# Stage end without a wait for stores, and another order of block 0, in a two-layer mixture-of-experts kernel

## The reference

```
# conditional part: one of 5 typed experts per sequence, two shared experts
s0, s1 = dense(x, swi[0], swo[0]), dense(x, swi[1], swo[1])
eo = relu(x @ wi[type]) @ wo[type]
gate_in = concat([eo[:, 0], s0[:, 0], s1[:, 0]])      # first token of each sequence
w = softmax(relu(gate_in @ g1) @ g2)                  # 3 weights per sequence
c = eo * w[0] + s0 * w[1] + s1 * w[2]
# then LN -> 16-head attention -> residual -> LN -> top-2 of 8 experts -> residual
```

## Time and profile before

| what | value |
|---|---|
| median of 3 runs | 601.53 us (599.89 to 604.56) |
| profiled execution | 602.28 us, its span 600.5 us |
| granted clock of TensorE, mean | 0.978 of full speed |
| typed experts end, layer one starts | 206 to 209 us |

### The profile page before, as it was taken

One profiled execution on the slowest core, in us unless ns is written; L12 is line 12 of the kernel. 1 busy time (PEld: TensorE's weight loads), 2 busy tenths in 40 slices (PEclk: granted clock), 3 DMA queues, 4 the chain that ended last, 5 costly groups with the idle time before them and its releaser, 6 DMA issues.

```text
span 600.5 us, 18671 instructions
## 1 busy us (share of the span) xinstructions
PE 540.4 (90%) x5852; PEld 464.3 (77%) x5853; DVE 395.9 (66%) x1440; ACT 372.9 (62%) x799; POOL 298.4 (50%) x308
## 2 busy tenths in 40 slices
PE   7979998788999979989999998998888889999991
PEld 3546665478999768778788887887777879999990
DVE  6988988963333324547587775778866546668782
ACT  2457778856666333655556755467777577888870
POOL 1387888651000068232375655257476575545541
PEclk9999999899999998999999999999999799999996
DMA  8931999423333111121453211032322222236364
GB/s 278 377 61 34 397 396 394 166 71 93 103 104 99 54 40 38 28 43 34 164 126 119 60 41 48 24 81 69 82 60 56 55 83 63 73 96 190 91 196 131
DMA packets 75774, 70.81 MB, mean 118 GB/s; under 512 B 26802, under 2 KB 63012, under 8 KB 75300
## 3 DMA queue, kind: packets, MB, share of 16 engines
q1 hardware_dynamic: 67968, 55.34, 29.9%
q0 software_dynamic: 6400, 13.19, 6.8%
q10 hardware_dynamic: 1316, 1.15, 0.6%
HBM read 30.19 MB, written 39.46 MB: 116 GB/s over the span
## 4 chain that ended last, share of the span: by engine, by line
PE 43%; issue 7%; POOL 6%; DVE 5%; DMA 1%; DVEq 1%; ACT 1%; ACTq 0%; POOLq 0%
PE u_py L1771 7%; PE u_py L1933 6%; PE u_pz L1914 6%; PE u_pg L1914 3%; PE u_pf L1933 3%; POOL u_eo_ew L1584 2%; PE u_pg L1814 2%; PE u_pz L1760 2%; PE u_pz L1762 2%; PE u_pg L1822 2%; PE u_pz L1761 2%; POOL rows_dram L1621 1%; PE u_pg L1836 1%; PE u_pe L1786 1%; PE u_pf L1792 1%
## 5 line engine op out<-in xcount | busy, mean ns | idle before, releaser
L1631 POOL DMA_INDIRECT y_dram<-u_hh,v_to x71 | 68.1, 960 | 59.6 <-DVE u_hh L2707 47.8
L1621 POOL DMA_INDIRECT rows_dram<-u_row,u_slots x64 | 62.8, 982 | 47.7 <-DVE u_slots L2577 31.2
L1771 PE MATMUL u_py<-cwo,u_hh 128*128 128x128 f32 x512 | 69.1, 282 | 3.9 <-DVE u_mid L2438 2.0
L1771 PEld LDWEIGHTS u_py<-cwo,u_hh 128*128 128x128 f32 x512 | 63.8, 194 | 8.7 <-issue 6.6
L1933 PE MATMUL u_py<-w,v_h 128*128 x384 | 53.3, 283 | 7.5 <-DVE u_hh L2707 4.3
L1933 PEld LDWEIGHTS u_py<-w,v_h 128*128 128x128 f32 x384 | 47.4, 194 | 10.2 <-issue 10.1
L1914 PE MATMUL u_pz<-v_xT,v_held 128*128 128x128 f32 x384 | 52.7, 283 | 2.7 <-DVE v_h L2687 2.1
L2159 ACT ACTIVATE u_hh<-u_pz 128x512 f32<-128x512 f32 x64 | 37.9, 595 | 27.7 <-PE u_pz L1762 24.8
L2232 ACT ACTIVATE v_held<-w 128x512 f32 x71 | 44.9, 633 | 12.4 <-PE u_pz L1914 3.8
L1914 PEld LDWEIGHTS u_pz<-v_xT,v_held 128*128 128x128 f32 x384 | 48.2, 198 | 3.9 <-issue 3.5
L2239 ACT ACTIVATE v_h<-u_pz,p_bT 128x128 f32<-128x128 f32 x124 | 36.6, 367 | 11.1 <-PE u_pz L1914 9.5
(11 more groups left out here) (386 smaller groups left out, 1493.0 us busy)
## 6 DMA issues: line engine op xcount, KB each, us to landing
rows_dram<-zero SPq DMA_DIRECT2D x1, 17160.0 KB
v_x<-rows_dram SPq DMA_DIRECT2D x71, 65.0 KB
w<-in_mw SPq DMA_DIRECT2D x2, 2048.0 KB
cwt<-in_cw SPq DMA_DIRECT2D x1, 2560.0 KB
xs_dram<-zero SPq DMA_DIRECT2D x1, 2240.0 KB, 13.0
e_xs<-xs_dram SPq DMA_DIRECT2D x35, 64.0 KB, 2.0
eo_dram<-e_y SPq DMA_DIRECT2D x35, 64.0 KB, 1.5
x_dram<-x SPq DMA_DIRECT2D x8, 256.0 KB
```

What stands on the lines that cost most here:

```text
L1621: pool.indirect_dma_start(rows_dram, bass.IndirectOffsetOnAxis(ap=slots[:, q, k, u:u + 1], axis=0), row[:, q, k, u, :], None).then_inc(sen ...
L1631: pool.indirect_dma_start(y_dram, bass.IndirectOffsetOnAxis(ap=vto[t % XR][:], axis=0), vy[:, t % XR, :], None).then_inc(v_sent[t % XR], 16)
L1771: last = nc.tensor.matmul(py[:, u * D:(u + 1) * D], hh[:, e % HR, u * P:(u + 1) * P], cwo[:, m * KF + k], start=(k == 0 and u == 0), stop= ...
```

## The change

Three things are changed. First, the three result buffers of the typed stage and their store semaphores now belong to the whole kernel; SP no longer waits for the stores at the stage's end, and POOL waits for them at the head of layer one, before the gate's gather. PE issues one unread matmul at the stage's end, not two. Second, the gate's gather lands in a buffer of `ew`, so gather(0) no longer waits for the gate's transpose, and POOL's order is gather(0), weigh(0), gather(1), gather(2), weigh(1), gather(3), carried(0), root1(0), weigh(2). Third, the gate's three steps move from step -1 into step 0 on PE and ACT. PE's order in block 0 is now: turn_x(0), an unread matmul, first e0, e1, e2, e3, gate 0, first e4, gate 1, second e0, gate 2, second e1, first e5, second e2, share, second e3, first e6, e7, turn_x(1), second e4, e5, e6, first e8, second e7, first e9, e10; step 1 is as before. ACT's is: ReLU e0, e1, e2, gate copy, ReLU e3, gate ReLU, ReLU e4, exponential, ReLU e5, e6, `high(1)`, ReLU e7, e8. DVE's is unchanged.

```diff
@@ -30,6 +30,7 @@
 TILE_UNROLL = 6
+YR = 3
 ET = (2 * T + E * (P - 1)) // P
@@ -93,9 +94,11 @@
 
-        kept = {"b_sent": ctx.enter_context(nc.semaphore("b_sent"))}
+        kept = {n: ctx.enter_context(nc.semaphore(n)) for n in ["b_sent"] + [f"e_stored{q}" for q in range(YR)]}
         sems, numbers = [ctx.enter_context(ExitStack())], []
         x1t = sb("x1t", [P, S, D])
+        typed_y = sb("typed_y", [P, YR, D])
+        typed_stored = [kept[f"e_stored{q}"] for q in range(YR)]
         ident = sb("ident", [P, P])
@@ -180,11 +183,11 @@
             typed_experts(nc, sb, pb, sem, ident, ones, tri, ln2, type_of_tile, x1_dram, x1t, xs_dram, eo_dram,
-                          cwt[:, 0:B_WO], cwt[:, B_WO:B_SWI], prep, spent)
+                          cwt[:, 0:B_WO], cwt[:, B_WO:B_SWI], prep, spent, typed_y, typed_stored)
         sems[0].close()
...
         layer_one(nc, a, sb, pb, sem, ident, ones, hmask, type_slot, x1t, eo_dram, v_dram, rows_dram, y_dram,
-                  cws, cwo, prep, expert_of_tile, row_of_tile, row_low, row_high, biases, out)
+                  cws, cwo, prep, expert_of_tile, row_of_tile, row_low, row_high, biases, typed_stored, out)
 
@@ -1123,9 +1126,9 @@
 
-def typed_experts(nc, sb, pb, sem, ident, ones, tri, ln2, type_of_tile, x1_dram, x1t, xs_dram, eo_dram, w1, w2, prep, spent):
-
-    U, V, R = TILE_UNROLL, 3, 3
+def typed_experts(nc, sb, pb, sem, ident, ones, tri, ln2, type_of_tile, x1_dram, x1t, xs_dram, eo_dram, w1, w2, prep, spent, y, stored):
+
+    U, V, R = TILE_UNROLL, 3, YR
     HF = FF // 2
@@ -1139,14 +1142,12 @@
         h = sb("e_h", [P, 2, FF], stack=st)
-        y = sb("e_y", [P, R, D], stack=st)
         pT = [pb(f"e_pT{q}", [P, 512], stack=st) for q in range(2)]
...
         w_held = sem("e_w_held", st)
-        stored = [sem(f"e_stored{q}", st) for q in range(R)]
         x_turned, xT_made, a_summed, c_summed, a_made, c_made, y_summed, y_made = (
@@ -1177,8 +1178,6 @@
                 sp.wait_ge(xt_loaded, 16 * NB)
-                for q in range(R):
-                    sp.wait_ge(stored[q], 16 * len(range(q, TT, R)))
 
@@ -1250,8 +1249,7 @@
                 rolled(pe, step, TT, U, 1)
-                for n in range(2):
-                    idle(pT[0], FF)
+                idle(pT[0], FF)
 
@@ -1341,7 +1339,7 @@
 def layer_one(nc, a, sb, pb, sem, ident, ones, hmask, type_slot, x1t, eo_dram, v_dram, rows_dram, y_dram,
-              cws, cwo, prep, expert_of_tile, row_of_tile, row_low, row_high, biases, out):
+              cws, cwo, prep, expert_of_tile, row_of_tile, row_low, row_high, biases, typed_stored, out):
 
@@ -1572,12 +1570,12 @@
             def _(pool):
-                pool.indirect_dma_start(eo[:, 0, 0, :], None, eo_dram,
+                for q in range(YR):
+                    pool.wait_ge(typed_stored[q], 16 * len(range(q, TT, YR)))
+                pool.indirect_dma_start(ew[:, 0, 0, :], None, eo_dram,
                                         bass.IndirectOffsetOnAxis(ap=type_slot[:, 0:1], axis=0)).then_inc(e0_loaded, 16)
...
                 def gather(i):
-                    if i == 0:
-                        pool.wait_ge(g_summed, 1)
                     after(pool, ew_made, i - 1)
@@ -1632,6 +1630,8 @@
                 for i in range(FIRST, NB):
+                    if i == -1:
+                        weigh(0)
                     if ok(i + 2):
@@ -1645,7 +1645,7 @@
                         scatter(i - 3, 0)
-                    if ok(i + 1):
+                    if ok(i + 1) and i != -1:
                         weigh(i + 1)
@@ -1724,11 +1724,11 @@
                 def gate(i, n):
-                    if i != -1:
+                    if i != 0:
                         return
...
                         pe.wait_ge(e0_loaded, 16)
-                        nc.tensor.transpose(pe_[:, 0:B], eo[:, 0, 0, :], ident[:]).then_inc(g_summed, 1)
+                        nc.tensor.transpose(pe_[:, 0:B], ew[:, 0, 0, :], ident[:]).then_inc(g_summed, 1)
                     elif n == 1:
@@ -1954,12 +1954,19 @@
                         first(i, 0, 3)
+                    gate(i, 0)
+                    if ok(i):
                         first(i, 1, 0)
+                    gate(i, 1)
                     if ok(i - 2):
...
                         second(i, 0, 0)
+                    gate(i, 2)
+                    if ok(i):
                         second(i, 0, 1)
+                    if i == 0:
+                        first(0, 1, 1)
                     if ok(i - 2):
@@ -1967,7 +1974,7 @@
                     share(i)
-                    if ok(i):
+                    if ok(i) and i > 0:
                         first(i, 1, 1)
@@ -1989,6 +1996,9 @@
                         attend(i - 2)
+                    if i == 0:
+                        first(0, 1, 3)
+                        turn_x(1)
                     if ok(i):
@@ -1999,13 +2009,13 @@
                         second(i, 1, 1)
-                    if ok(i + 1):
+                    if ok(i + 1) and i != 0:
                         turn_x(i + 1)
...
                         project(i - 2)
-                    if ok(i):
+                    if ok(i) and i > 0:
                         first(i, 1, 3)
@@ -2015,11 +2025,8 @@
                         first(i + 1, 0, 1)
-                    gate(i, 0)
                     if ok(i + 1):
                         first(i + 1, 0, 2)
-                    gate(i, 1)
-                    gate(i, 2)
                 turn_p(NB - 2, 0)
```

## The result

The changed kernel takes 606.74 us (median of 12 runs, 605.68 to 609.56) against 602.31 us for the kernel before. The ratio is 1.0094 with an interval of 1.0073 to 1.0116: 5.7 us slower (4.4 to 7.0). Forecast was 2.5 us slower. The sign was right and the two mechanisms that were forecast came, but the size was more than twice the forecast: one of their terms was too small, and a third cost, a stop of PE further on, was not in the sum. A few executions, in a slower state of the chip, are left out of every ratio and mean.

The account below looks back on a forecast made before the run. It took PE and POOL's list to be tied up to turn_normed(0), with POOL late next. Root +1.0 and clock +1.5 gave +2.5 us: 604.8 profiled, 604.0 us forecast as median, range 599.5 to 607.5.

Parts of the forecast that it names:

- the two mechanisms that were forecast: In block 0, root1(0) on POOL ends 1.0 us later, and PE's clock halves around its long wait, costing 1.5 us.
- The stage's end: At the typed stage's end, SP is done 1.3 us earlier and PE starts layer one 1.3 us earlier (bounds 0 and 1.3).
- POOL's list and the gate: In block 0, `wtok` comes at 218.5 us, 2.4 us earlier; root1(0) ends 19.5 us after it, 1.0 us later than before.
- The clock: Around PE's 8 us wait before turn_normed(0), a half-clock fall of 3.4 us costs 1.5 us (bounds 0 and 3.4).
- a longer fall: Rival: PE's clock fall costs 3.4 us, or also slows block 1's firsts; 606 us, 14%.
- The sum: Whole kernel: +1.0 us for the root and +1.5 for the clock make +2.5 us, nothing added or given back after 240 us.
- The rival that ends faster: PE keeps its lead of 5.0 us in block 0 because POOL's list shortens; 596.5 us, 6%.

Follow-up runs that it names:

- the filled wait: The changed kernel with eight more unread matmuls that PE issues in front of turn_normed(0), where it waits; ratio to the kernel before 1.0040 (1.0014 to 1.0066).
- both moves on POOL: The changed kernel with gather(1) put back in front of weigh(0) and gather(3) moved behind root1(0); ratio to the kernel before 0.9922, again 0.9942.
- the two timed controls: A second unread matmul of 128 columns at the stage's end, added to the changed kernel (1.0100) and to that kernel with gather(1) earlier and gather(3) later (0.9924).
- gather(1) first: The changed kernel with gather(1) put back in front of weigh(0) on POOL; ratio to the kernel before 0.9999 (0.9971 to 1.0027).

## Why the prediction was off

- **The stage's end**: right in its size, 1.1 to 1.3 us of earlier start; the gate's gather gained 0.3 to 0.6. PE's second matmul had to go for it, as said. But the traces with that end show 1.0 to 1.6 us more at PE's stop in block 1, 1.6 in the changed kernel. This cost stood in the sum at nothing. The step that failed is "from 240 us on every list is as before and PE is nearly always busy, so I find nothing that gives the delay back, or adds to it": PE's list is the same from there, yet PE stops longer in it, with one instruction fewer in front. (That this is its place among the instruction fetches is argued, not shown.) The kernel before has such stops as well, 1.70 us behind block 0's attend, 1.01 there and 1.94 us 78 us later; I had not read them.
- **POOL's list and the gate**: right. `wtok` 11.17 us behind PE's start against 11.1 forecast, the root 19.3 behind weigh(0) against 19.5, turn_normed(0) 1.0 us later, counted from the first typed result (66.3 + 30.3 before, 65.2 + 32.5 after), against 1.0. PE's wait was 7.8 for 8.
- **The clock**: the mis-sized term. I took a fall of 3.4 us, the length of the one in block 0 before, and 1.5 us of loss. It began inside the long wait, lasted 10.2 us, covered the first 5.8 us of the work behind the wait and cost 2.7 us, which the filled wait shows by itself. The bound of 3.4 us held it; of the cases listed the rival "a longer fall" (606 us, given 14%) is the nearest. That its time is also near the measured one is in part luck, since it has no stop of 1.6 us in it.
- **The sum**: 1.0 + 2.7 + 1.6 = 5.3 us, in place of 1.0 + 1.5. Measured were 5.7, 4.9 and 5.6. The range of 599.5 to 607.5 held the time.
- **The rival that ends faster** was rightly given little: with POOL's order as changed, PE's lead of 5 us is wasted. With both moves on POOL it is kept: scores(0, 0) comes 6.1 us earlier than before.
- **The rule of the Trainium skill** ("TensorE: Matmul & The Clock Gate", Part 1), that activity alone releases the throttled state and that half of the throttled time is lost, was on the right side: 5.8 us of work at half the clock, 2.7 us lost. Taking the fall's length, 3.4 us, from a wait of 2 us was my error: with the wait of 7.8 us it was 6.8 or 10.2 us in all seven traces.

Left open is whether the timed price of the changed stage end, 1 to 2 us above what the chain up to scores(0, 0) gives, is the stop alone. The traces say so; the two timed controls say so only once the low clock's time is taken off, and within their noise.

## What to carry to other kernels

Before reordering an in-order engine, find the list that the next stage's first step waits for, and count what stands in front of that step in that list; here five microseconds of gathers that nobody needed yet stood in front of a reciprocal root of one microsecond, and moving them gave 0.6 to 0.8% where the change had lost 0.9%. When a reordering gathers TensorE's short waits into one long wait, count what the clock does behind it: here waits of 1.7 to 2.9 us cost nothing to 1.7 us at the low clock, and the wait of 7.8 us cost 1.3 to 2.8. Removing an instruction from a long unrolled list can move a stop elsewhere in it, so read the "issue" waits of the whole span before and after.

## What was not expected of the hardware

A wait of 7.8 us on TensorE was followed by 5.5 to 6.0 us of work at the low clock in four of seven traces, and by 2.9 to 4.3 us in the other three. A wait of 2.9 us (gather(1) first) was followed by none, and one of 2.2 us by a fall that cost 1.6 us (8.57 against 6.98). The length of the wait alone does not tell whether the clock falls, nor how long it stays low. One matmul fewer in PE's list went with a stop some 80 to 90 us further on that was 2.0 to 2.6 us long instead of at most 1.01, in nine traces of ten. The duration of layer zero up to the first typed result varied from 140.9 to 143.8 us between executions.
